# Extra TensorE products of constants at the start of each batch of a graph network with routed FFN

## The chip, the cores and the metric

The kernel runs on one core of a Trainium2 chip. The engines named here are PE (TensorE, with its weight loads as PEld), DVE (VectorE), ACT (ScalarE), POOL (GpSimd) and SP (SyncE, which issues most of the DMAs). The metric is the time on the device in microseconds (us). Three timed runs of the kernel before have a median of 739.09 us (737.73 to 739.27).

## The reference

The input x has 8 batches of 1024 rows and 128 features, and every batch has its own 1024 x 1024 adjacency matrix of zeros and ones. What is computed, cut to its core:

```
# graph layer: maximum over a row's first 25 neighbours
xn    = layernorm(x)
idx   = the first S=25 columns with adj != 0, in rising order
agg   = max over idx of xn[idx]     (also max with 0 if the row has at most 25 neighbours)
x     = x + relu(concat(xn, agg) @ W + b)

# FFN with routed experts; each tile of 128 rows has one route
h0    = layernorm(x)
h     = relu(h0 @ Wi.T + bi)
for l in 0, 1:
    h = relu(h @ Ws[l].T + bs[l]  +  h @ Wr[l, e].T + br[l, e]  +  h)    # e = the tile's route
out   = x + h @ Wo.T + bo
```

## The kernel before

**Tiling and stages.** A batch is 8 tiles of 128 rows. Tile 0, whose rows have the most neighbours, has its rows fetched by indexed DMAs that POOL issues. For the other 7 tiles (896 columns) the kernel works with slots. A slot is a group of source rows and a rank r within the group: a matrix with a one where a row's r-th neighbour of that group is (the one-hot, made by DVE or ACT from an array `rank`) is multiplied on PE with the normalised features, which are split in two parts, and DVE takes the maximum of the product with what it has (`fold_slot`, lines 959 and 961). There are 44 slots to a batch. A full slot is 4 matmuls (512 and 384 columns, for two parts), one with a group of two tiles 8, a narrow one 2.

**The order of the work.** Every engine's program walks over stages s = 0 to 9 and in each over positions p = 0 to 43 (`positions`). In stage s there run: slot p of batch s-1 (`slot`), the graph layer's end and the FFN of batch s-2 (`finish`), and masks, ranks and one-hots of batch s (`prepare`). Everything is in the order that this walk writes; an engine executes its list in that order and waits on semaphores. So there are eight stages with slots (s = 1 to 8), and in seven of them (s = 2 to 8) an FFN runs too; stage 9 has only the last batch's FFN.

**Around the change**, in a stage from 2 on:
- PE: slot p waits for its one-hot (`s_acthot` or `s_onehot`) and for the fold of slot p-2 (`s_max`), since there are two accumulators. In `finish`, position 0 turns the features (line 765), 2 to 5 hold the graph layer's product (lines 784 and 785), 12 and 13 turn h0 (line 792, waits for `s_h0` from ACT), 14 to 17 multiply with Wi (line 799, waits for ACT's copies), 19 to 34 are the two expert layers (line 815).
- DVE: the fold of slot p, then one-hots for slots 4 ahead, then its part of `finish` (the sum with x at positions 4 and 6, statistics one position later), then `norm_pair`: the layernorm chain at positions 7 and 8 (lines 980 to 991), which goes to ACT for a square root (`std`) and comes back. The fold of slot 8 stands between the halves of that chain.
- ACT: at position 7 it waits for DVE's variance, then h0 in two halves at positions 9 and 11 (line 587), copies of the turned tiles at 12 and 13 (line 593), the first layer's relu at 14 to 17 (line 597), and one-hots for slots 5 ahead in between (lines 645, 656 and 662).
- `prep_ps[0]` and `prep_ps[1]` are two PSUM banks that `prepare` uses for ranks (line 842). In stages from 1 on that is at positions 16 to 38, so that nothing is in them at the positions before. ACT reads them out (line 616) and signals `s_q`.
- `down` is a table of constants, 128 x 1024 of 16 bit, which POOL writes once at the start.

Of the kernel before, what the change touches and what calls it, by code (L numbers as in the profile page):

```python
# [15 lines left out]
P = 128  # L16
# [45 lines left out]
def gnn_ffn_program(nc, x, adj, gnn_W, gnn_b, route_id, Wi, bi, Wr, br, Ws, bs, Wo, bo, out):  # L62
    B, N, C = x.shape
    IT = N // P
# [10 lines left out]
    BANK = 512  # L75
# [8 lines left out]
    CONSTS = 7  # L84
    assert HUBS == 1 and sorted(PLACES) == [(g, r) for g in range(NG) for r in range(1, CAPS[g][0] + 1)]
    assert NW == 34 and HC == 2 and L == 2 and all(w == TT for _, _, w in SLOTS[0:2])


# [22 lines left out]
    VERDICT_AT = 24  # L111
    SPLIT_AFTER, SPLIT_BATCH = 35, 4
    FIRST_W_AT = 6
    OUT_AT = {36: 0, 39: 1}
    WEIGHTS_AT = [] + [NS + p for p in (
        0, 1, 2, 3, 4, 5, 6, 7, 9, 10, 11, 12, 14, 15, 16, 18, 19, 20, 22, 23, 24, 25,
# [14 lines left out]
    with ExitStack() as ctx:  # L131
        def sb(name, shape, dt=F32):
            return ctx.enter_context(nc.sbuf_tensor(name, shape, dt))
# [4 lines left out]
        def sem(name):  # L138
            return ctx.enter_context(nc.semaphore(name))
# [5 lines left out]
        down = sb("down", [P, N], F16)  # L145
# [74 lines left out]
        prep_f = [p[:, :].bitcast(F32) for p in prep_ps]  # L220
# [29 lines left out]
        s_q = sem("s_q")  # L250
# [61 lines left out]
        def positions():  # L312

            for s in range(B + 2):
                for p in range(NS):
                    yield s, p
# [22 lines left out]
        def weights_at(s, p, late):  # L339
            at_ = s * NS + p - late  # L340
            return [m for m in range(NW) if WEIGHTS_AT[m] == at_]
# [28 lines left out]
        def _(sp):  # L370
# [6 lines left out]
            def load_expert(k, i):  # L377

                e = sp.value_load(route[0:1, k * IT + i:k * IT + i + 1], min_val=0, max_val=NE)
                sp.dma_start(wst[:, i, :], folded[bass.ds(e, 1)].rearrange("a p w -> (a p) w")).then_inc(s_w[i], 16)  # L380
# [16 lines left out]
            for s, p in positions():  # L397
                k = s - 2
                if k == 0 and 0 <= p - FIRST_W_AT < IT:
                    if p == FIRST_W_AT:  # L400
                        sp.wait_ge(s_route, 1)
                        for i in range(NST):
                            sp.wait_ge(s_wstore[i], 16 * len(range(i, NW, NST)))
                        sp.wait_ge(s_bstore, 16)
                    load_expert(0, p - FIRST_W_AT)
                if s < B:
# [43 lines left out]
                if 0 <= k < B:  # L450
# [6 lines left out]
                    if p - 1 in LAYER_AT[1] and k + 1 < B:  # L457
                        i = LAYER_AT[1][p - 1]
                        sp.wait_ge(s_r[1], k * IT + i + 1)
                        load_expert(k + 1, i)  # L460
                    if p - 1 in OUT_AT:
                        g = OUT_AT[p - 1]
                        sp.wait_ge(s_y, 2 * k + g + 1)
# [263 lines left out]
        def _(pe):  # L727
            pe.wait_ge(s_const, CONSTS)

            def start_with_bias(bank, which):  # L730
                pe.matmul(bank, onesb[0:SPLITS, :], bias_rows[:, which].rearrange("p t c -> p (t c)"),
                          start=True, stop=False)

            def slot(b, p):
                n = b * NS + p
                g, r, wide = SLOTS[p]
                first, many = GROUPS[g]
                if p == 0:
                    pe.wait_ge(s_split, b + 1)
                if p in ACT_HOT:  # L740
                    pe.wait_ge(s_acthot, b * len(ACT_HOT) + ACT_HOT.index(p) + 1)
                else:
                    pe.wait_ge(s_onehot, b * len(DVE_HOT) + DVE_HOT.index(p) + 1)
                if n >= 2:
                    pe.wait_ge(s_max, n - 1)
                for j in range(many):
                    for part in range(PARTS):
                        for c0 in range(0, wide * P, BANK):
                            c1 = min(c0 + BANK, wide * P)
                            mm = pe.matmul(slot_ps[n % 2][:, c0:c1], xsplit[:, b % 2, part, first + j, :],  # L750
                                           onehot[:, UNIT[n] + j, c0:c1], start=(j == 0 and part == 0),
                                           stop=(j == many - 1 and part == PARTS - 1))
                mm.then_inc(s_slot, 1)

            def finish(k, p):
# [46 lines left out]
                for l in range(L):  # L802
                    if p in LAYER_AT[l]:
# [13 lines left out]
                        mm.then_inc(s_l[l], 1)  # L817
                if p in OUT_AT:
                    g = OUT_AT[p]
                    pe.wait_ge(s_r[1], k * IT + 7 + g)  # L820
# [8 lines left out]
            def prepare(s, p):  # L829
                if p in RANK_AT[s > 0]:  # L830
                    jt = RANK_AT[s > 0][p]
                    second = [f for f, many in GROUPS if many == 2 and f + 1 == jt]
                    for c in range(CHUNKS):
                        if jt == 0:
                            for i, many in enumerate(turns((s + 1) * TT)):
                                pe.wait_ge(s_turn[i], 16 * many)
                            if s > 0:
                                pe.wait_ge(s_q, 2 * IT * s - 1 + c)
                        else:
                            pe.wait_ge(s_q, 2 * IT * s + 2 * jt + c - 1)  # L840
                        cols = slice(c * CW, (c + 1) * CW)
                        mm = pe.matmul(prep_f[c][:, 0:CW], before[:, :], at[:, jt, cols],  # L842
                                       start=True, stop=not second)
                        if second:
                            mm = pe.matmul(prep_f[c][:, 0:CW], onesb[:, :], at[:, jt - 1, cols],
                                           start=False, stop=True)
                        mm.then_inc(s_rank, 1)
# [11 lines left out]
            for s, p in positions():  # L859
                if 1 <= s <= B:  # L860
                    if s == 1 and p == 0:
                        pe.wait_ge(s_biases, 1)
                    slot(s - 1, p)
                if 2 <= s:
                    finish(s - 2, p)
                if s < B:
                    prepare(s, p)
                if (s, p) == (B + 1, VERDICT_AT):
                    pe.wait_ge(s_above, 1)
                    pe.matmul(prep_f[0][0:1, 0:ROWS], above[:, 0:1], ident[0:ROWS, 0:ROWS], start=True,  # L870
                              stop=True).then_inc(s_overs, 1)
                for m in weights_at(s, p, 0):
                    if m < NIN:
                        pe.wait_ge(s_wfirst[m // 4], 16 * 4)
                    else:
                        pe.wait_ge(s_wload[m % NIN], 16 * (m // NIN))
                    if m >= 2:
                        pe.wait_ge(s_wfold, m - 1)
                    for kc in range(HC):
                        for hc in range(HC):  # L880
                            mm = pe.transpose(ffn_ps[m % 2][:, (kc * HC + hc) * P:(kc * HC + hc + 1) * P],  # L881
                                              w_in[m % NIN][:, hc, kc * P:(kc + 1) * P], ident[:, :])
                    mm.then_inc(s_wT, 1)
# [42 lines left out]
        def _(dve):  # L926
# [201 lines left out]
            def finish(k, p):  # L1128
# [9 lines left out]
                if p - 1 in SUM_AT:  # L1138
                    g = SUM_AT[p - 1]
                    dve.wait_ge(s_sum, 2 * k + g + 1)  # L1140
                    for i in range(4 * g, 4 * g + 4):
                        dve.bn_stats(stats[:, 1, i, :], x1[:, i, :])  # L1142
                if p - 1 in OUT_AT:
                    g = OUT_AT[p - 1]
                    dve.wait_ge(s_o, 2 * k + g + 1)
# [119 lines left out]
```

## Time and profile before

| | |
|---|---|
| median of 3 runs | 739.09 us |
| the profiled execution, own time | 739.0 us |
| its span | 737.3 us |
| PE busy | 612.4 us (83%) |
| DVE busy | 605.3 us (82%) |
| ACT busy | 567.5 us (77%) |
| POOL busy | 238.0 us (32%) |
| PE share of the chain that ended last | 61%, DVE 21% |
| mean granted clock of TensorE | 0.933 |

PE, DVE and ACT are busy for nearly the same time, so no average tells which one holds the others up; that has to be read stage by stage. The granted clock is given as a share of the full 2.4 GHz: 1.00 is 2.4 GHz, 0.50 is 1.2 GHz, and a value between is a stretch that held both. PE is called busy while a matmul is in flight, with an end that is modelled, so that a row's time is some tenths of a microsecond longer than the columns take.

### The profile page before, as it was taken

The numbers are of one execution on the slowest core, as the hardware profiler recorded it, in microseconds if no ns is written. First come the engines' busy times: TensorE is split into PE (matmuls) and PEld (weight loads), VectorE is DVE, ScalarE is ACT, GpSimd is POOL, SyncE is SP. The second block draws the span as 40 slices with busy tenths as digits, with TensorE's granted clock in tenths as the row PEclk, the third lists the DMA queues.
The fourth block names the chain that finished last, engine by engine and source line by source line (L and its number), as shares of the span: only waits on it lengthen the run. The fifth ranks groups of instructions, "written<-read, shape, count | busy, mean of one in ns | idle before, by whom it ended". The sixth has DMA issues, their size and how long they took to land.

```text
span 737.3 us, 11826 instructions
## 1 busy us (share of the span) xinstructions
PE 612.4 (83%) x3496; PEld 500.2 (68%) x3497; DVE 605.3 (82%) x1047; ACT 567.5 (77%) x1053; POOL 238.0 (32%) x260
## 2 busy tenths in 40 slices
PE   0463766688999799979997999899987999799786
PEld 0052545466988588858975797669875888588665
DVE  3766799988998898889988898899888988777740
ACT  5683364489998898889988998899889997488162
POOL 4522224533243332434242334333343234510000
PEclk9998798998999799979998899989998999799989
DMA  9999996479746965497639764795475553135222
GB/s 295 326 191 285 283 369 185 135 175 297 222 136 152 270 175 161 109 232 220 174 106 214 230 176 138 169 264 161 120 183 126 152 139 93 33 103 142 58 74 75
DMA packets 145171, 131.73 MB, mean 179 GB/s; under 512 B 72219, under 2 KB 112324, under 8 KB 145092
## 3 DMA queue, kind: packets, MB, share of 16 engines
q1 hardware_dynamic: 128124, 105.94, 53.5%
q0 software_dynamic: 7296, 15.74, 8.5%
q10 hardware_dynamic: 9680, 9.21, 4.4%
q8 instruction: 31, 0.51, 0.3%
q14 instruction: 40, 0.33, 0.1%
HBM read 98.20 MB, written 17.98 MB: 158 GB/s over the span
## 4 chain that ended last, share of the span: by engine, by line
PE 61%; DVE 21%; DMA 5%; issue 5%; ACT 4%; SPq 2%; DVEq 2%; ACTq 0%
PE slot_ps L750 29%; PE ffn_ps L815 15%; DVE acc L961 9%; PE prep_ps L842 3%; DMA at<-mask 3%; PE ffn_ps L799 3%; PE ffn_ps L825 2%; DMA adj_sb<-in_adj_dram 2%; PE ffn_ps L784 2%; DVE onehot L948 2%; PE ffn_ps L765 2%; DVE gath L1039 2%; DVE wst L1126 1%; PE ffn_ps L785 1%; DVE stats L1142 1%
## 5 line engine op out<-in xcount | busy, mean ns | idle before, releaser
L750 PE MATMUL slot_ps<-onehot,xsplit 128*128 128x512 f32 (+3 forms) x1376 | 373.4, 399 | 46.7 <-DVE acc L961 42.5
L961 DVE TENSOR_TENSOR acc<-slot_ps,acc 128x896 f32<-128x896 f32 (+2 forms) x336 | 293.9, 883 | 51.6 <-PE slot_ps L750 49.4
L750 PEld LDWEIGHTS slot_ps<-onehot,xsplit 128*128 128x128 f32 x1376 | 250.3, 204 | 103.2 <-issue 71.1
L530 POOL DMA_INDIRECT gath<-feature_table,idx x200 | 202.2, 1011 | 363.0 <-DMA gath<-feature_table,idx 273.5
L645 ACT ACTIVATE away<-rank,ranks 128x896 bf16<-128x896 bf16 (+3 forms) x168 | 133.0, 792 | 6.6 <-DVE wst L1126 6.3
L815 PE MATMUL ffn_ps<-hT,wst 128*128 128x128 f32 x1024 | 135.5, 277 | 0.6
L662 ACT ACTIVATE onehot<-away 128x896 fp32r<-128x896 bf16 (+3 forms) x168 | 118.7, 707 | 21.7 <-PE slot_ps L750 10.3
L815 PEld LDWEIGHTS ffn_ps<-hT,wst 128*128 128x128 f32 x1024 | 128.5, 191 | 8.2 <-issue 3.5
L604 ACT ACTIVATE hT<-ffn_ps,wst 128x128 f32<-128x128 f32 x256 | 82.4, 384 | 19.3 <-PE ffn_ps L815 17.4
L948 DVE TENSOR_SCALAR onehot<-rank,ranks 128x896 fp32r<-128x896 bf16 (+3 forms) x128 | 94.8, 741 | 2.4 <-PE slot_ps L750 2.4
L616 ACT ACTIVATE rank<-prep_ps 128x448 bf16<-128x448 f32 x128 | 63.1, 552 | 22.6 <-PE prep_ps L842 10.6
L656 ACT ACTIVATE onehot<-rank,ranks 128x896 fp32r<-128x896 bf16 (+1 forms) x56 | 66.0, 1179 | 11.4 <-PE slot_ps L750 10.7
L689 ACT ACTIVATE mask<-adj_sb 128x1024 bf16<-128x1024 uint32 x56 | 58.0, 1046 | 16.2 <-DMA at<-mask 12.1
L842 PE MATMUL prep_ps<-at,before 128*128 128x448 bf16 x128 | 40.3, 384 | 15.9 <-DMA at<-mask 12.3
L881 PE MATMUL ffn_ps<-ident,hT 128*128 128x128 f32 x136 | 24.9, 314 | 33.7 <-DVE wst L1126 31.3
L881 PEld LDWEIGHTS ffn_ps<-ident,hT 128*128 128x128 f32 x136 | 17.9, 162 | 43.2 <-issue 42.1
L1020 DVE MAX8 top<-score 128x8 f32<-128x1024 f32 x32 | 39.1, 1220 | 0.3
L799 PE MATMUL ffn_ps<-xnT,wiT 128*128 128x512 f32 x64 | 33.3, 608 | 0.2 <-ACT xnT L593 0.2
L842 PEld LDWEIGHTS prep_ps<-at,before 128*128 128x128 bf16 x128 | 11.4, 99 | 32.1 <-DMA at<-mask 11.7
L825 PE MATMUL ffn_ps<-woT,hT 128*128 128x128 f32 x256 | 32.8, 281 | 0.0
L825 PEld LDWEIGHTS ffn_ps<-woT,hT 128*128 128x128 f32 x256 | 29.8, 191 | 3.6 <-issue 3.6
L515 POOL TENSOR_TENSOR xsplit<-xn,xsplit 128x1024 fp32r<-128x1024 f32 x8 | 19.2, 2400 | 38.7 <-DVE acc L961 31.2
(120 smaller groups left out, 541.9 us busy)
## 6 DMA issues: line engine op xcount, KB each, us to landing
wst<-folded_weights SPq DMA_DIRECT2D x128, 257.0 KB, 2.9
adj_sb<-in_adj_dram SPq DMA_DIRECT2D x64, 512.0 KB, 5.9
folded_weights<-wst ACTq DMA_DIRECT2D x34, 256.0 KB, 5.8
hT<-in_L_ffn_Wr_dram SPq DMA_DIRECT2D x26, 256.0 KB, 8.8
xs<-in_x_dram SPq DMA_DIRECT2D x8, 512.0 KB, 8.0
feature_table<-xn SPq DMA_DIRECT2D x8, 512.0 KB, 4.2
x<-in_x_dram SPq DMA_DIRECT2D x8, 512.0 KB, 4.2
out_dram<-h SPq DMA_DIRECT2D x16, 256.0 KB, 2.5
```

Source lines behind the costliest of these rows:

```text
L530: pool.indirect_dma_start(gath[:, j, :], None, tables[b], bass.IndirectOffsetOnAxis(ap=idx[:, b % 2, h, j:j + 1], axis=0)).then_inc(signal ...
L604: ins = act.activation(hT[:, 1 - l, j, i, :], ffn_ps[(i + 1) % 2][:, j * P:(j + 1) * P], ACT.Relu, bias=wst[:, i, HC * HID + j:HC * HID + ...
L616: act.activation(rank[:, s % 2, jt, c * CW:(c + 1) * CW], prep_f[c][:, 0:CW], ACT.Copy, bias=float(NONE)).then_inc(s_q, 1)
L645: act.activation(away[:, i % AWAYS, 0:wide * P], rank[:, b % 2, first, 0:wide * P], ACT.Square, bias=ranks[:, r - 1:r], scale=-1.0).then_i ...
L656: act.activation(onehot[:, UNIT[n]:UNIT[n] + many, 0:wide * P], rank[:, b % 2, first:first + many, 0:wide * P], ACT.Relu, bias=ranks[:, 1: ...
L662: act.activation(onehot[:, UNIT[n], 0:wide * P], away[:, i % AWAYS, 0:wide * P], ACT.Relu, bias=1.0, scale=-1.0).then_inc(s_acthot, 1)
L750: mm = pe.matmul(slot_ps[n % 2][:, c0:c1], xsplit[:, b % 2, part, first + j, :], onehot[:, UNIT[n] + j, c0:c1], start=(j == 0 and part == ...
L815: mm = pe.matmul(ffn_ps[(i + 1) % 2][:, j * P:(j + 1) * P], wst[:, i, c0:c0 + P], hT[:, l, kc, i, :], start=(kc == 0), stop=(kc == HC - 1))
L825: mm = pe.matmul(o, hT[:, 0, kc, i, :], woT[:, kc, :], start=False, stop=(i % 4 == 3 and kc == HC - 1))
L842: mm = pe.matmul(prep_f[c][:, 0:CW], before[:, :], at[:, jt, cols], start=True, stop=not second)
L948: dve.tensor_scalar(onehot[:, UNIT[n]:UNIT[n] + many, 0:wide * P], rank[:, b % 2, first:first + many, 0:wide * P], ranks[:, r - 1:r], None ...
L961: dve.tensor_tensor(acc[:, p % 2, 0:cols], slot_ps[n % 2][:, 0:cols], acc[:, p % 2, 0:cols], ALU.max).then_inc(s_max, 1)
```

## The change

At positions 5 to 11 of the stages 2 to 8, ahead of the position's slot, PE multiplies a 128 x 128 piece of `down` with a 128 x 512 piece of it into `prep_ps[0]`: 2, 4, 5, 5, 4, 3 and 2 times, 25 in a stage. Nobody reads the result. The first of them waits for `s_q`, that is, for ACT to have read the last ranks of the stage before. In stage 9 there are 24 such matmuls at positions 6 to 11, behind `finish`. Together they are 7 x 25 + 24 = 199.

```
+    BUSY_AT = {5: 2, 6: 4, 7: 5, 8: 5, 9: 4, 10: 3, 11: 2}
+    BUSY_AT_END = {6: 4, 7: 4, 8: 4, 9: 4, 10: 4, 11: 4}
...
+            def keep_busy(s, p):
+
+                where = BUSY_AT if s < B + 1 else BUSY_AT_END
+                if p == min(where):
+                    pe.wait_ge(s_q, 2 * IT * min(s, B))
+                for _ in range(where.get(p, 0)):
+                    pe.matmul(prep_f[0][:, 0:BANK], down[:, 0:P], down[:, 0:BANK], start=True, stop=True)
...
                 if 1 <= s <= B:
                     if s == 1 and p == 0:
                         pe.wait_ge(s_biases, 1)
+                    if s >= 2:
+                        keep_busy(s, p)
                     slot(s - 1, p)
                 if 2 <= s:
                     finish(s - 2, p)
+                if s == B + 1:
+                    keep_busy(s, p)
```

Lines below the new ones have moved: in the kernel after, 750 is 760, and 784, 785 and 792 are 794, 795 and 802.

PE's program before, in a stage from 2 on, from the slot of position 5 to that of position 8 (784 and 785 are the graph layer, 750 the slots):

```order
L750 MATMUL slot_ps<-onehot,xsplit 128x512 [waits s_max,s_onehot]
L750 MATMUL slot_ps<-onehot,xsplit 128x384
L750 MATMUL slot_ps<-onehot,xsplit 128x512
L750 MATMUL slot_ps<-onehot,xsplit 128x384
L784 MATMUL ffn_ps<-gw,xnT 128x128
L785 MATMUL ffn_ps<-gw,aggT 128x128
L784 MATMUL ffn_ps<-gw,xnT 128x128
L785 MATMUL ffn_ps<-gw,aggT 128x128
L750 MATMUL slot_ps<-onehot,xsplit 128x384 [waits s_max,s_acthot]
L750 MATMUL slot_ps<-onehot,xsplit 128x384
L750 MATMUL slot_ps<-onehot,xsplit 128x512 [waits s_max,s_onehot]
```

The same place now, from the graph layer of position 5 to the start of slot 8 (742 is a product of constants):

```order
L794 MATMUL ffn_ps<-gw,xnT 128x128
L795 MATMUL ffn_ps<-gw,aggT 128x128
L742 MATMUL prep_ps<-down 128x512 x4
L760 MATMUL slot_ps<-onehot,xsplit 128x384 [waits s_max,s_acthot]
L760 MATMUL slot_ps<-onehot,xsplit 128x384
L742 MATMUL prep_ps<-down 128x512 x5
L760 MATMUL slot_ps<-onehot,xsplit 128x512 [waits s_max,s_onehot]
L760 MATMUL slot_ps<-onehot,xsplit 128x384
L760 MATMUL slot_ps<-onehot,xsplit 128x512
L760 MATMUL slot_ps<-onehot,xsplit 128x384
L742 MATMUL prep_ps<-down 128x512 x5
L760 MATMUL slot_ps<-onehot,xsplit 128x512 [waits s_max,s_acthot]
```

Ahead of slots 6, 7 and 8 there now stand 4, 5 and 5 matmuls; two more stand ahead of slot 5, above this piece.

PE's program in stage 9, from the graph layer's last products to the turning of h0, before:

```order
L784 MATMUL ffn_ps<-gw,xnT 128x128
L785 MATMUL ffn_ps<-gw,aggT 128x128
L792 MATMUL ffn_ps<-ident,h 128x128 [waits s_h0]
L792 MATMUL ffn_ps<-ident,h 128x128 x3
L792 MATMUL ffn_ps<-ident,h 128x128 [waits s_h0]
```

And now:

```order
L795 MATMUL ffn_ps<-gw,aggT 128x128
L742 MATMUL prep_ps<-down 128x512 [waits s_q]
L742 MATMUL prep_ps<-down 128x512 x23
L802 MATMUL ffn_ps<-ident,h 128x128 [waits s_h0]
L802 MATMUL ffn_ps<-ident,h 128x128 x3
```

All 24 stand in one piece, behind the graph layer and ahead of the wait for h0. No other engine's program changes.

## Rows read from the trace of the kernel before

**Rows 1.** The page: granted TensorE clock in 40 slices, in tenths.
```profile
PEclk9998798998999799979998899989998999799989
```
**Rows 2.** Chain of waits, start and length in us: position 0 of three stages.
```profile
382.67 1.74 PE ffn_ps L765 x16
...
460.61 1.74 PE ffn_ps L765 x16
...
537.71 1.74 PE ffn_ps L765 x16
```
**Rows 3.** Busy time and clock (ninth column) by 2 us, stage from 382.67.
```profile
398.00:400.00 2.00, 0.48 (x1) 0.50 (x2) 1.77 (x6) 1.59 (x4) 0.62 (x1) 0.83 1.25 281
400.00:402.00 2.00, 1.90 (x6) 1.15 (x4) 1.78 (x6) 1.56 (x4) 1.27 (x2) 0.50 1.02 327
...
408.00:410.00 2.00, 2.00 (x9) 1.76 (x8) 1.51 (x2) 2.00 (x5) 0.54 (x1) 0.61 1.05 377
```
**Rows 4.** Timeline of DVE, folds of slots 5, 6, 7 and 8.
```profile
392.55 1.09 DVE L961 TENSOR_TENSOR acc<-slot_ps,acc 128x896 f32<-128x896 f32 x1 [0.80 <-PE slot_ps L750]
...
394.34 0.54 DVE L961 TENSOR_TENSOR acc<-slot_ps,acc 128x384 f32<-128x384 f32 x1
...
395.40 1.08 DVE L961 TENSOR_TENSOR acc<-slot_ps,acc 128x896 f32<-128x896 f32 x1
...
398.29 1.08 DVE L961 TENSOR_TENSOR acc<-slot_ps,acc 128x896 f32<-128x896 f32 x1
```
**Rows 5.** Timeline of DVE, fold of slot 13 in stages 2 to 8.
```profile
174.33 1.09 DVE L961 TENSOR_TENSOR acc<-slot_ps,acc 128x896 f32<-128x896 f32 x1 [1.92 <-PE slot_ps L750]
...
252.31 1.09 DVE L961 TENSOR_TENSOR acc<-slot_ps,acc 128x896 f32<-128x896 f32 x1 [1.81 <-PE slot_ps L750]
...
330.41 1.09 DVE L961 TENSOR_TENSOR acc<-slot_ps,acc 128x896 f32<-128x896 f32 x1 [1.80 <-PE slot_ps L750]
...
408.49 1.09 DVE L961 TENSOR_TENSOR acc<-slot_ps,acc 128x896 f32<-128x896 f32 x1 [2.02 <-PE slot_ps L750]
...
485.60 1.09 DVE L961 TENSOR_TENSOR acc<-slot_ps,acc 128x896 f32<-128x896 f32 x1 [1.35 <-PE slot_ps L750]
...
563.35 1.09 DVE L961 TENSOR_TENSOR acc<-slot_ps,acc 128x896 f32<-128x896 f32 x1 [2.00 <-PE slot_ps L750]
...
641.61 1.09 DVE L961 TENSOR_TENSOR acc<-slot_ps,acc 128x896 f32<-128x896 f32 x1 [2.69 <-PE slot_ps L750]
```
**Rows 6.** Timeline of PE in the same stage: slots 6+7, 10+11, 12; Wi; ranks.
```profile
393.16 1.68 PE L750 MATMUL slot_ps<-onehot,xsplit 128*128 128x384 f32 x6
...
399.52 2.59 PE L750 MATMUL slot_ps<-onehot,xsplit 128*128 128x512 f32 x6 [2.31 <-DVE acc L961]
403.63 0.98 PE L750 MATMUL slot_ps<-onehot,xsplit 128*128 128x384 f32 x2 [1.52 <-DVE acc L961]
...
409.67 1.02 PE L799 MATMUL ffn_ps<-xnT,wiT 128*128 128x512 f32 x2
...
413.88 0.54 PE L842 MATMUL prep_ps<-at,before 128*128 128x448 bf16 x2
```
**Rows 7.** Line 842 from 412 to 417 us, ns minimum/median/maximum.
```profile
L842 PE MATMUL prep_ps<-at,before x4: 352/352/363, 413.9 to 417.0; 128*128 128x448 bf16 x4
```
**Rows 8.** Timeline of ACT in the same stage: square root, copy of turned h0.
```profile
398.41 0.22 ACT L678 ACTIVATE std<-mv 128x16 f32<-128x16 f32 x1 [2.50 <-DVE mv L986]
...
408.03 0.58 ACT L593 ACTIVATE xnT<-ffn_ps 128x512 f32<-128x512 f32 x1
```
**Rows 9.** Timeline of PE in stage 9.
```profile
702.41 1.11 PE L792 MATMUL ffn_ps<-ident,h 128*128 128x128 f32 x4 [6.19 <-ACT h L587]
...
703.95 1.12 PE L792 MATMUL ffn_ps<-ident,h 128*128 128x128 f32 x4 [0.42 <-ACT h L587]
```
**Rows 10.** Busy time and clock by 2 us in stage 9.
```profile
704.00:706.00 2.00, 2.00 (x6) 1.45 (x7) 1.43 (x7) 0.98 (x2) 0.00 (x0) 0.50 0.00 0
706.00:708.00 2.00, 2.00 (x4) 0.54 (x4) 1.70 (x5) 1.07 (x2) 0.00 (x0) 0.87 0.01 4
```

## The prediction

> **What bounds the kernel now.** I read the page's clock line first. It dips about once every four slices, so once a stage [rows 1]. The table by 2 us then places a dip: in the stage that begins at 382.67 us the clock is whole until inside 398 to 400, at half from there, and whole again inside 408 to 410 [rows 3]. From the shares 0.83 and 0.61 the half rate lasts from 399.3 to 409.6 us. Just before the fall PE had waited 2.31 us, and in the half-rate stretch it waits another 1.52 us, both times for DVE's folds [rows 6].
>
> The timeline of DVE shows who pays. DVE waits 0.80 us ahead of the fold of slot 5, then works without a gap until it waits 2.02 us for slot 13, which PE was computing at half rate [rows 4, 5]. After that it is busy nearly without a gap through the middle of the stage. So in stages 2 to 7 a late fold 13 is a late stage. The trace has a test of this: the stage from 460.61 has the shortest wait there, 1.35 us [rows 5], and lasts 537.71 - 460.61 = 77.10 us against 460.61 - 382.67 = 77.94 for the one before it [rows 2]. What is saved ahead of fold 13 is kept. The six waits of stages 2 to 7 are 1.92, 1.81, 1.80, 2.02, 1.35 and 2.00, together 10.9 us, and stage 8 has 2.69 [rows 5].
>
> **What an added matmul costs.** No row shows this one. The nearest is line 842: two 16-bit matmuls of 448 columns take 0.54 us, one takes 0.35 [rows 6, 7], so the second begins 0.19 us after the first, and 512 columns take 0.19 x 512/448 = 0.217 us at the whole clock. At half rate it would be twice that. The range for one is 0.21 (512 columns at 2.4 GHz) to 0.43. I take 0.217; weight loads of 16 bit lie beside the matmul before.
>
> **Part 1: the 25 in stages 2 to 7.** They stand ahead of each slot's waits, so where PE would wait for DVE they fill the wait, and where PE was in time they make the slot late. I follow the stage from 382.67.
> - Fold 5 was already waiting for PE. Two matmuls make it 0.43 us late: 392.98.
> - Slot 7 ended at 393.16 + 1.68 = 394.84. Ahead of it now stand 2 + 4 + 5 = 11 matmuls, 2.38 us. The six matmuls of slots 6 and 7 have 2560 columns, 1.07 us at 2.4 GHz; of the 0.6 us left about 0.3 is a wait for fold 5 (to 392.55 + 1.09 = 393.64), which the matmuls cover. So slot 7 ends at 394.84 + 2.38 - 0.3 = 396.9, and fold 7 starts at 397.0 in place of 395.40: 1.6 us late.
> - The five ahead of slot 8 end at 396.7 + 1.08 = 397.8, slot 8 needs some 1.0 and is done at 398.8. Fold 8 now comes at 398.29 + 1.6 = 399.9, so it isn't delayed further. The same holds for 9 to 11: 4, 3 and 2 matmuls run inside waits of PE.
> - DVE has no gap from fold 5 to fold 12, so all that follows is 1.6 us late, and it is ready for fold 13 at 408.49 - 2.02 + 1.6 = 408.1.
> - With the clock whole, PE ends slot 13 at about 407.7: slot 12 starts behind fold 10, now at 403.63 [rows 6] and then at 405.2; its own 768 columns take 0.33, the turning of h0 0.43, and 1.5 + 0.2 for the eight matmuls of slot 13. So fold 13 starts at 408.1 in place of 408.49.
>
> A stage so gains its wait less 1.6 us: over six stages 10.9 - 9.6 = 1.3 us.
>
> Against it stands ACT. Its square root waits for DVE [rows 8] and is 1.6 us late too, and ACT has no gap behind it, so the copy of turned h0 begins at 409.6 and ends at 410.2 in place of 408.6. PE's line 799 then starts at 410.25, not 409.67 [rows 6]. Followed on through line 799, this makes slot 17 about 0.25 us late for DVE; behind it the order has slack again. Six times 0.25 is 1.5 us. Part 1 with a whole clock is therefore 1.5 - 1.3 = +0.2 us: what the clock gives, the late norm takes.
>
> **Part 2: the 25 in stage 8.** There DVE and ACT have less to do and PE bounds the rest of the stage. DVE is ready for fold 13 at 641.61 - 2.69 + 1.6 = 640.5; PE comes at about 640.7. Gain 0.9 us.
>
> **Part 3: the 24 in stage 9.** PE waits 6.19 us for h0 [rows 9]; 24 x 0.217 = 5.2 us lie inside that wait, and they cost nothing (at the half rate they would take 10.4 and cost 4). With the clock whole, what ran at half rate from 703.95 until inside 706 to 708 (share 0.87, so until 706.5) [rows 9, 10] takes half: 2.55/2, about 1.25 us gained, since all behind it hangs on it.
>
> **Part 4: a clock that falls all the same.** Slot 10 waits for the end of fold 8 (399.9 + 1.1 = 401.0) and takes 0.8, the two matmuls behind it 0.43: 402.2. From there to slot 12 at 405.2 PE has only slot 11's two small matmuls, a hole of 3.0 us. It is like those of 2.31 and 1.52 us ahead of and behind the falls now [rows 6]. When it does make the clock fall, that is at about 405 to 406, and slots 12 and 13 and the turning of h0 (2.3 us of work) run at half rate for the most part: fold 13 is then some 1.1 us later than in part 1, and since that takes away ACT's 0.25, the stage costs 0.85 more. I give a fall 4 in 10 in each of seven stages: 2.8 x 0.85 = +2.4 us.
>
> Waits and queues: the new wait for s_q is met, since ACT's last rank of a stage is at position 38 and this is position 5 of the next. POOL, SP and DMAs get no instruction. The masks of positions 7, 9 and 10 are up to 1.6 us later with ACT, and their transposes; the ranks that need them are at 413.88 [rows 6], some 3 us behind.
>
> **Sum.** 739.0 (the profiled execution, 737.3 of span and 1.7 around it; 0.1 under the median) + 0.2 - 0.9 - 1.25 + 2.4 = 739.4 us.
>
> **Two rules of the Trainium skill.** In the trace the clock is at half for about 10 us a stage after PE's waits [rows 3, 6]. The page TensorE: Matmul & The Clock Gate (What's actually happening) says that the throttled state is the default and that activity releases it. By that the added work would hold the clock in every stage and the sum loses part 4: 737.0. The rows can't show whether products nobody needs count.
> The trace shows slots in program order. The same page (Part 2, on weight loads) says that matmuls stay in program order and only weight loads are pulled ahead; by that the eleven ahead of slot 7 are all paid, as in part 1. If they gave way, the 9.6 us and the 1.5 would go.
>
> **The rivals.**
> - *The clock never falls.* For: stage 460.61 kept what it saved. Against: the hole at 402.2. Time: 739.0 + 0.2 - 0.9 - 1.25 = 737.0; with ACT's 0.25 not arising, 735.5. If the matmuls also lay wholly in waits (fold 5's wait of 0.80 and gapless DVE speak against it), 10.9 + 2.7 + 1.25 would go: 724.
> - *Slower: the matmuls ahead of slot 7 push back DVE's norm chain and with it ACT by more than the fold-13 wait is worth.* The place is slots 5 to 7, the price (delay - wait) a stage. It decides from a delay of about 2 us. A matmul of 0.25 us, or 0.1 us each time PE turns between 16-bit and 32-bit work, makes the delay 1.9 to 2.0 (0.35 x 6: +2 us); with falls in more than half of the stages, +1 more: 742. At 0.43 us each the delay would be 1.6 + 2.4 = 4.0 us, six times 4.0 - 1.8: 752.
> - *No effect of the matmuls on the clock.* Falls stay where they were, and slot 12 with all behind it is 1.6 us late at the same rate: 739.0 + 7 x 1.6 = 750. Nothing in the trace speaks for it, but it doesn't show such products either.
>
> **How the numbers follow.** Forecast (delay 1.6, falls in some stages): 0.43, its own range 738 to 741. Clock never falls: 0.27 (737, to 735.5), fully free 0.03. Longer delay: 0.22 (742). No effect on the clock: 0.05. The range 735.8 to 742.5 leaves out the far cases. About 0.2% (1.5 us) is what a measurement of this kernel can tell from no change. Below 737.6: the free case, most of the cases in which the clock never falls and a few of the forecast's, 0.31. Above 740.6: 0.05 + 0.22 and a share of the forecast's upper end, 0.29. Between: 0.40.
>
> **What would show it.** In the profile after: fold 7 about 4.0 us behind the start of fold 5 in place of 395.40 - 392.55 = 2.85 [rows 4], fold 13 with a wait under 0.3 us where the clock holds; ACT's std wait 4.1 us instead of 2.5; line 742 at 0.22 us each; the clock whole in stage 9, and its products with Wi over 1.25 us earlier. The forecast is wrong if fold 7 is not late (then far faster), if the clock line has a dip in each stage still (slower), or if DVE has new waits behind fold 13.

## The result and the profile after

The kernel after takes 743.88 us (median of 9 runs, 740.87 to 746.84), the kernel before 739.09 us (median of 9, 736.87 to 741.72). The ratio is 1.0065 with a 95% interval of 1.004 to 1.009: slower, by 3.0 to 6.6 us. The forecast of 739.4 us and its range up to 742.5 were wrong. The profiled execution of the kernel after is the fastest of its nine, 740.87 us with a span of 739.1. Four executions of the experiments' timings took between 910 and 2022 us, in a slow state of the chip, and are left out of every ratio.

The page of the kernel after, its clock line and two groups of matmuls (the added ones and the product with Wi):

```profile
PEclk9986898999999999999999999999999999999999
...
L742 PE MATMUL prep_ps<-down 128*128 128x512 f16 x199 | 51.5, 381 | 0.0
...
L809 PE MATMUL ffn_ps<-xnT,wiT 128*128 128x512 f32 x64 | 33.1, 605 | 7.1 <-ACT xnT L595 4.7
```

Against [rows 1] the dips are gone from stage 2 on: in this execution the 199 matmuls hold the clock. But line 809 (799 before) now has 7.1 us of idle time in front of it, where the kernel before had 0.2.

The chain of waits of the kernel after: position 0 of stages 2 to 9, each row the start of a stage.

```profile
147.74 1.74 PE ffn_ps L775 x16
226.48 1.74 PE ffn_ps L775 x16
305.21 1.73 PE ffn_ps L775 x16
383.92 1.73 PE ffn_ps L775 x16
462.48 1.74 PE ffn_ps L775 x16
541.06 1.73 PE ffn_ps L775 x16
619.39 1.74 PE ffn_ps L775 x16
692.11 1.75 PE ffn_ps L775 x16
```

The same view of the kernel before, the three starts that [rows 2] doesn't show and that bound the stretches compared here:

```profile
226.67 1.74 PE ffn_ps L765 x16
...
615.52 1.73 PE ffn_ps L765 x16
688.96 1.75 PE ffn_ps L765 x16
```

Three stretches come out of the two. Stages 3 to 7: 619.39 - 226.48 = 392.91 us against 615.52 - 226.67 = 388.85, so +4.06, or 0.81 a stage. Stage 8: 72.72 against 73.44, so -0.72. From the start of stage 9 to the end of the span: 46.95 against 48.31, so -1.36. Of the stretches compared, only the middle stages lose.

DVE in the stage from 383.92, folds 5, 6, 7, 8, 13, 15, 17 and 19 of the kernel after:

```profile
394.22 1.09 DVE L975 TENSOR_TENSOR acc<-slot_ps,acc 128x896 f32<-128x896 f32 x1 [1.23 <-PE slot_ps L760]
396.31 0.56 DVE L975 TENSOR_TENSOR acc<-slot_ps,acc 128x384 f32<-128x384 f32 x1 [0.23 <-PE slot_ps L760]
398.23 1.09 DVE L975 TENSOR_TENSOR acc<-slot_ps,acc 128x896 f32<-128x896 f32 x1 [0.76 <-PE slot_ps L760]
401.13 1.08 DVE L975 TENSOR_TENSOR acc<-slot_ps,acc 128x896 f32<-128x896 f32 x1
...
409.05 1.08 DVE L975 TENSOR_TENSOR acc<-slot_ps,acc 128x896 f32<-128x896 f32 x1
...
413.43 1.09 DVE L975 TENSOR_TENSOR acc<-slot_ps,acc 128x896 f32<-128x896 f32 x1 [0.25 <-PE slot_ps L760]
...
417.16 1.09 DVE L975 TENSOR_TENSOR acc<-slot_ps,acc 128x896 f32<-128x896 f32 x1 [0.32 <-PE slot_ps L760]
...
420.87 1.09 DVE L975 TENSOR_TENSOR acc<-slot_ps,acc 128x896 f32<-128x896 f32 x1 [0.42 <-PE slot_ps L760]
```

From fold 5 to fold 7 it is 4.01 us, where [rows 4] have 2.85, and fold 5's own wait is 1.23 where it was 0.80: together 1.6 us. Fold 8 follows without a wait. Fold 13 has no wait, where [rows 5] have 2.02. Then there are three waits for PE, 0.25, 0.32 and 0.42, together 0.99 us (0.72 to 0.92 in the other five of stages 2 to 7). The kernel before has none at these folds in the same stage; its folds 15, 17, and 18 with 19:

```profile
412.55 1.09 DVE L961 TENSOR_TENSOR acc<-slot_ps,acc 128x896 f32<-128x896 f32 x1
...
415.87 1.09 DVE L961 TENSOR_TENSOR acc<-slot_ps,acc 128x896 f32<-128x896 f32 x1
...
418.06 2.08 DVE L961 TENSOR_TENSOR acc<-slot_ps,acc 128x896 f32<-128x896 f32 x2
```

PE in that stage, timeline of the kernel after (slot 12, the second turning of h0, and the product with Wi):

```profile
406.29 0.58 PE L760 MATMUL slot_ps<-onehot,xsplit 128*128 128x384 f32 x2 [1.65 <-DVE acc L975]
...
409.27 0.65 PE L802 MATMUL ffn_ps<-ident,h 128*128 128x128 f32 x4 [0.32 <-ACT h L589]
...
411.45 1.12 PE L809 MATMUL ffn_ps<-xnT,wiT 128*128 128x512 f32 x2 [1.18 <-ACT xnT L595]
```

ACT in the same stage, square root and copy of the turned h0:

```profile
401.25 0.22 ACT L680 ACTIVATE std<-mv 128x16 f32<-128x16 f32 x1 [4.11 <-DVE mv L1000]
...
410.83 0.58 ACT L595 ACTIVATE xnT<-ffn_ps 128x512 f32<-128x512 f32 x1
```

ACT waits 4.11 us for the norm where [rows 8] have 2.50: the 1.6 us again. From the square root to the copy it takes 9.6 us in both kernels (401.25 to 410.83; 398.41 to 408.03), so it catches nothing up. PE waits 1.18 us for the copy, and line 809 starts 27.5 us into the stage (411.45 - 383.92), where it was 27.0 (409.67 - 382.67). (Counted from the first fold it is 26.05 us here, and 24.4 to 25.5 over stages 2 to 7 of the kernel before.) From there PE's timeline has no gap until past slot 19: PE is what DVE waits for.

PE in stage 9 of the kernel after:

```profile
699.20 5.34 PE L742 MATMUL prep_ps<-down 128*128 128x512 f16 x24
705.56 0.66 PE L802 MATMUL ffn_ps<-ident,h 128*128 128x128 f32 x4 [1.01 <-ACT h L589]
707.10 0.66 PE L802 MATMUL ffn_ps<-ident,h 128*128 128x128 f32 x4 [0.88 <-ACT h L589]
```

The 24 matmuls take 5.34 us, 0.22 each, inside the wait for h0, which still has 1.01 us left of the 6.19 of [rows 9].

### The profile page after: what moved, and what is told of

It reads as the page before. It is cut to its first block, busy times and chain, and to the rows that moved or that the text cites. A ratio compares the mean times of both kernels' runs of the same rounds, so it can differ in the third digit from the quotient of the medians.

```text
span 739.1 us, 12224 instructions
## 1 busy us (share of the span) xinstructions
PE 630.9 (85%) x3695; PEld 503.1 (68%) x3696; DVE 607.3 (82%) x1047; ACT 565.9 (77%) x1053; POOL 237.6 (32%) x260
## 4 chain that ended last, share of the span: by engine, by line
PE 63%; DVE 17%; ACT 7%; issue 5%; DMA 4%; DVEq 2%; SPq 1%; ACTq 0%
PE slot_ps L760 28%; PE ffn_ps L825 14%; DVE acc L975 7%; PE ffn_ps L809 4%; PE prep_ps L852 3%; ACT h L589 3%; PE ffn_ps L835 2%; PE ffn_ps L794 2%; PE prep_ps L742 2%; DMA at<-mask 2%; PE ffn_ps L795 2%; PE ffn_ps L775 2%; ACT mask L691 2%; DMA adj_sb<-in_adj_dram 2%; DVE wst L1140 2%
## 5 line engine op out<-in xcount | busy, mean ns | idle before, releaser
L760 PE MATMUL slot_ps<-onehot,xsplit 128*128 128x512 f32 (+3 forms) x1376 | 362.7, 389 | 29.4 <-DVE acc L975 24.6
L760 PEld LDWEIGHTS slot_ps<-onehot,xsplit 128*128 128x128 f32 x1376 | 241.9, 194 | 80.8 <-issue 50.1
L658 ACT ACTIVATE onehot<-rank,ranks 128x896 fp32r<-128x896 bf16 (+1 forms) x56 | 66.0, 1179 | 11.5 <-PE slot_ps L760 10.7
L852 PE MATMUL prep_ps<-at,before 128*128 128x448 bf16 x128 | 40.2, 384 | 15.0 <-DMA at<-mask 11.4
L742 PE MATMUL prep_ps<-down 128*128 128x512 f16 x199 | 51.5, 381 | 0.0
L680 ACT ACTIVATE std<-mv 128x16 f32<-128x16 f32 (+1 forms) x10 | 2.1, 214 | 43.8 <-DVE mv L1000 39.0
L852 PEld LDWEIGHTS prep_ps<-at,before 128*128 128x128 bf16 x128 | 11.4, 99 | 30.8 <-DMA at<-mask 11.5
```

The source lines that it names most:

```text
L658: act.activation(onehot[:, UNIT[n]:UNIT[n] + many, 0:wide * P], rank[:, b % 2, first:first + many, 0:wide * P], ACT.Relu, bias=ranks[:, 1: ...
L742: pe.matmul(prep_f[0][:, 0:BANK], down[:, 0:P], down[:, 0:BANK], start=True, stop=True)
```

## The experiments

Each kernel was timed beside runs of the kernel before on the same chip; the ratio is to those. Not all experiments ran on the same chip: the runs of the kernel before have medians of 739.7 us beside the first four, 739.1 beside the next four and 737.3 beside the last two, so kernels of different groups are compared by ratio or by stages and not by their times alone. "Line 809" is the start of the product with Wi behind the first fold of its stage, "the stage" the distance of such first folds; both are typical of stages without a fall of the clock. The theories: **A**, the 11 matmuls ahead of slot 7 delay DVE's norm chain by 1.6 us, ACT with it, and PE waits for ACT; **B**, the early matmuls are what holds the clock; **C**, any added matmul costs.

**Late products only.**

```
-    BUSY_AT = {5: 2, 6: 4, 7: 5, 8: 5, 9: 4, 10: 3, 11: 2}
+    BUSY_AT = {8: 5, 9: 4, 10: 3, 11: 2}
```

> The products at positions 5, 6 and 7 are left out, those at 8 to 11 and in stage 9 stay. Theory A (the 11 products ahead of slot 7 make DVE's norm chain 1.6 us late, ACT with it, and PE then waits 1.2 us for ACT's copy of the turned h0): fold 7 is back at 11.2 us behind the stage's first fold, PE's wait at line 809 is gone, and if the clock still holds the stage is about 1.8 us shorter than in the kernel before (DVE's wait for slot 13 goes): 6 x 1.8 + 1.5 + 1.25, about 727 us. Theory B (the early products are what holds the clock): fold 7 is in time, but the clock falls once a stage again, and the time is that of the kernel before less the end, 738 us. Theory C (any added product costs, wherever it stands): over 741 us.

734.03 us, ratio 0.9937 (0.9908 to 0.9966): faster than the kernel before. The fold of slot 13 comes without a wait, and line 809 still waits for ACT. Timeline of DVE, then of PE, in the stage from 383.70 (first fold at 385.19):

```profile
407.44 1.07 DVE L975 TENSOR_TENSOR acc<-slot_ps,acc 128x896 f32<-128x896 f32 x1
```

```profile
409.63 1.12 PE L809 MATMUL ffn_ps<-xnT,wiT 128*128 128x512 f32 x2 [1.17 <-ACT xnT L595]
```

Fold 7 is back at 11.2 us behind the first fold, line 809 starts at 24.4 in place of 26.05, and the stages are 76.7 to 77.4 us in place of 78.3 to 78.75. Removing 11 matmuls a stage moved fold 7 and line 809 by the same 1.6 us. C falls, since 14 a stage stay, and B for the most part: the clock is whole in four of seven stages without the early products. A is right on the delay, but wrong on one point: the wait at line 809 did not go. It is 1.17 us here too, because PE and ACT's copy are both 1.6 us earlier; with the clock held, it is ACT's copy that sets line 809. So the time came out 7 us above the 727 of A (whose own sum, taken from 739.1, gives 725.5). The clock fell in stages 4, 6 and 7, each time ahead of slot 12, for one stretch of 3.4 us. Busy time and clock of this kernel by 2 us (clock in the ninth column):

```profile
326.00:328.00 2.00, 0.92 (x5) 0.91 (x6) 2.00 (x4) 2.00 (x4) 0.59 (x1) 0.90 0.59 131
328.00:330.00 2.00, 2.00 (x8) 1.81 (x7) 1.92 (x3) 2.00 (x6) 1.70 (x2) 0.50 0.82 156
330.00:332.00 2.00, 2.00 (x10) 1.55 (x9) 0.65 (x1) 2.00 (x5) 0.04 (x1) 0.74 1.07 168
```

**Early products only.**

```
-    BUSY_AT = {5: 2, 6: 4, 7: 5, 8: 5, 9: 4, 10: 3, 11: 2}
+    BUSY_AT = {5: 2, 6: 4, 7: 5}
```

> The products at positions 8 to 11 are left out, those at 5 to 7 and in stage 9 stay. Theory A: the delay of 1.6 us at fold 7 and PE's wait for ACT stay whole, and the clock may fall again behind position 8; stages of 78.7 us or more, and with falls 79.5: 744 to 749 us. Theory B: the clock holds as in the kernel after, and the time is the same within 1 us. Theory C: 14 fewer products in seven stages give back about 14 x 0.217 x 7 = 21 us at most; anything under 740 us would speak for it.

746.84 us, ratio 1.0115 (1.008 to 1.0149), inside A's range. Fold 7 is at 12.8 us, and the clock falls in each of stages 2 to 8, so B falls here too. Chain of waits, the longest stage's start and the next:

```profile
227.91 1.74 PE ffn_ps L775 x16
307.64 1.74 PE ffn_ps L775 x16
```

That stage is 79.73 us long; stages 2 to 7 take 78.4 to 79.7. The delay without the held clock is worse than either kernel.

**Stage 9 only.**

```
-                    if s >= 2:
+                    if s >= B + 2:
                         keep_busy(s, p)
```

> Only the 24 products in stage 9 stay; the stages 2 to 8 are as before. Theory A: stages like before (about 78.0 us, clock falls in each), the end shorter by the half-rate stretch: 1.25 us under the kernel before. Theory C: no gain or a loss of up to 4 us there.

738.09 us, ratio 0.9987 (0.9964 to 1.0009). The stages are like before (76.9 to 78.05), and from the start of stage 9 to the end it is 736.1 - 689.04 = 47.1 us against 48.3. Its row in the chain of waits:

```profile
689.04 1.75 PE ffn_ps L775 x16
```

The time alone can't tell 1.2 us from nothing; the stretch in the profile shows it.

**ACT's normalised tiles later, in the kernel after.**

```
-             [11, 13, 14, 16]]
+             [13, 14, 16, 17]]
```

> The kernel after, with ACT's four pairs of normalised tiles moved from positions 11, 13, 14 and 16 to 13, 14, 16 and 17, so that one pair (0.87 us) no longer stands between h0 and the copies of the turned h0. Theory A (the loss is PE's wait for ACT's copy at line 809): the copy starts 0.8 us earlier, the wait of 1.2 us shrinks to about 0.4, and each of six stages is about 0.7 us shorter: 4 us under the kernel after. Rival (DVE's 1.6 us are the loss by themselves, or PE is full anyway): no change within 1 us.

742.81 us, ratio 1.0053 (1.0023 to 1.0084), 1.1 us under the kernel after. The median is unclear, the profile isn't. Chain of waits, starts of stages 2 to 5:

```profile
148.30 1.74 PE ffn_ps L775 x16
226.37 1.73 PE ffn_ps L775 x16
305.36 1.74 PE ffn_ps L775 x16
383.46 1.74 PE ffn_ps L775 x16
```

Stages 2 and 4 are 78.07 and 78.10 us, against 78.7 in the kernel after: 0.6 less (0.7 was expected), and line 809 starts at 25.3 in place of 26.05. The wait for ACT went from 1.18 to 0.41 us. PE in stage 4:

```profile
332.13 1.12 PE L809 MATMUL ffn_ps<-xnT,wiT 128*128 128x512 f32 x2 [0.41 <-ACT xnT L595]
```

The stage between them is 78.99, because here the clock fell in stages 3, 5, 7 and 8 (in none in the kernel after), each time ahead of slot 12 for 3.4 us. So a fall costs 0.9 us here (0.7 in stage 5, whose length is 78.81), and in stage 8, whose length is 74.00 us against 72.7 in the kernel after, 1.3. A move of ACT's operations, which changes the program of neither PE nor DVE, gains what it takes from ACT's path: this is the run that shows ACT in the path. That the clock would fall in four stages was not foreseen. They have all 25 products of the kernel after, so these do not hold the clock in every case; why it fell here stays open.

**Late products and six at position 12.**

```
-    BUSY_AT = {5: 2, 6: 4, 7: 5, 8: 5, 9: 4, 10: 3, 11: 2}
+    BUSY_AT = {8: 5, 9: 4, 10: 3, 11: 2, 12: 6}
```

> Products at positions 8 to 11 as in the kernel after (5, 4, 3, 2), none at 5 to 7, and 6 more at position 12, ahead of slot 12, where PE waits 1.65 us for DVE's fold 10; stage 9 as in the kernel after. Theory A with falls priced at 0.85 us each (the clock fell for 3.4 us in three stages of the run with late products, each time in the hole ahead of slot 12): no fall in any stage from 2 on, all stages near 77.0 us, 1 to 3 us under the run with late products alone, 731 to 733 us. Rival (6 x 0.217 = 1.3 us more in front of slot 12 push slot 13 back): DVE waits for slot 13 and the time is that of late products or above.

732.46 us, ratio 0.9915 (0.9878 to 0.9951). No fall from stage 2 on, and stages of 76.7 to 77.2 us. Timeline of PE:

```profile
407.95 1.13 PE L809 MATMUL ffn_ps<-xnT,wiT 128*128 128x512 f32 x2 [1.17 <-ACT xnT L595]
```

Line 809 starts at 24.45 and waits for ACT as before. The three falls of the run with late products cost it only some 0.4 us in all: its stages with a fall take 77.40, 77.07 and 76.73 us, the same ones here 77.13, 76.97 and 76.72. PE had the wait for ACT to spare (it is down to 0.12 to 0.24 us in those stages). So the gain of the six is small, and the intervals of the two ratios overlap.

**Narrow products.**

```
-                    pe.matmul(prep_f[0][:, 0:BANK], down[:, 0:P], down[:, 0:BANK], start=True, stop=True)
+                    pe.matmul(prep_f[0][:, 0:P], down[:, 0:P], down[:, 0:P], start=True, stop=True)
```

> The kernel after with every product cut from 512 to 128 columns, the same count (25 a stage, 24 in stage 9). Theory A (the delay is the columns streamed ahead of slot 7): one product takes about 0.06 us, the 11 ahead of slot 7 about 0.6 us less the 0.3 of wait that they cover, so that fold 7 is 0.1 to 0.5 us late in place of 1.6. With so little work the clock falls once a stage as before: about 738 to 741 us. Rival (a fixed price for each product, whatever its width): fold 7 stays 1.6 us late, and the time is 745 us or more.

741.72 us, ratio 1.0032 (1.0006 to 1.0058), 0.7 above the expected. Fold 7 is at 11.4 us behind the first fold, 0.17 late: the price is the columns, not the count. The clock fell once in each of stages 2 to 8 and in stage 9 (mean 0.929), so these products hold nothing. In the profiles stages 2 to 8 take 540.2 us, as in the kernel before; the end behind them takes 49.9 against 48.5 (both from the first product of line 775, 765 before). The fall in stage 9 begins 3 us later there, at 702.6 us in place of 699.7, and so lies over more of the work behind the wait for h0; that this is the whole loss was not tested.

**ACT's normalised tiles later, in the kernel before** (the edit of the fourth experiment, no products).

> The kernel before, with ACT's pairs of normalised tiles moved from positions 11, 13, 14 and 16 to 13, 14, 16 and 17 and no products. Theory A: PE is behind ACT there because of the half-rate slot 13, so ACT's copy is not what it waits for, and nothing changes: within 1 us of the kernel before. Rival (moving the pairs is a gain by itself): 3 us or more under the kernel before.

738.89 us, ratio 0.9994 (0.9968 to 1.002). Nothing changes, as A has it: without the held clock PE is late at line 799 by itself, and ACT's copy isn't waited for.

**The kernel after again.**

> The kernel after, once more, for a second profile and for times beside the others. Its profiled run had no fall in stages 2 to 9 and is 3 us under the median of its runs. If that difference is falls in the hole ahead of slot 12 (0.85 us each), this profile is either again without falls near 741 us, or shows falls of 3.4 us behind position 11 and stages of 79.4 to 79.6 us with them. If it is anything else, stages without a fall are longer than 78.8 us.

743.8 us, ratio 1.0062 (1.0033 to 1.009). Chain of waits, starts of stages 2, 3, 8 and 9:

```profile
151.18 1.74 PE ffn_ps L775 x16
229.68 1.74 PE ffn_ps L775 x16
...
622.69 1.74 PE ffn_ps L775 x16
695.39 1.75 PE ffn_ps L775 x16
```

Its span is 742.5 us, 3.4 above the other profile's, and no clock fall lies in stages 2 to 8, nor in stage 9 before its last microseconds. From stage 2 to the end it is 591.3 us in both. The whole difference of the two executions lies ahead of stage 2 (151.18 against 147.74), where there are no products. Neither of the two explanations in the expectation holds.

**Late products with 12, and ACT's tiles later.** Both edits together.

> Late products with 6 at position 12, and ACT's pairs of normalised tiles at positions 13, 14, 16 and 17. Theory A (with the clock held, the stage is as long as the start of line 809, the product with Wi, is late, and that waits for ACT's copy): the start goes from 24.45 us behind the stage's first fold to about 23.7, and the stages from 77.0 to 76.2 to 76.5 us: 728 to 730 us. Rival (DVE, without a gap from fold 5 to fold 14, is the bound once the delay is gone): line 809 starts earlier and the stages stay at 76.9 to 77.1 us, 732 us.

730.29 us (median of 6), ratio 0.9896 (0.9863 to 0.993), the lowest ratio here; its interval overlaps that of the kernel without ACT's move. PE in the stage from 376.12 (first fold at 377.62):

```profile
401.55 1.13 PE L809 MATMUL ffn_ps<-xnT,wiT 128*128 128x512 f32 x2 [0.40 <-ACT xnT L595]
```

Line 809 starts at 23.65 in most stages (23.93 in this one) and the stages are 76.2 to 76.7 us, in place of 24.45 and 76.7 to 77.2. Stage by stage it is 0.3 to 0.6 us, 2.8 us over the six. The wait for ACT went from 1.17 to 0.4 us. The profiled execution has a span of 723.7 us, 7.0 below that of the kernel without the move; 4.3 of this is that stage 2 starts at 146.4 in place of 150.7, so that its stages are what is compared.

**Late products with 12, and the five of position 7.**

```
-    BUSY_AT = {5: 2, 6: 4, 7: 5, 8: 5, 9: 4, 10: 3, 11: 2}
+    BUSY_AT = {7: 5, 8: 5, 9: 4, 10: 3, 11: 2, 12: 6}
```

> Late products with 6 at position 12, and the five of position 7 as well (none at 5 and 6). Theory A: slot 7 was done 0.55 us ahead of its fold and had about 0.3 us of wait, so of the 5 x 0.217 = 1.08 us about 0.2 to 0.3 us reach fold 7, which starts at 11.4 to 11.5 us behind the stage's first fold; the start of line 809 and the stages are later by the same amount, 77.2 to 77.3 us, and the time is 1 to 2 us above that of late products with 12. Rival (the first products ahead of fold 7 cost in full, or the price is not linear in the delay): fold 7 is 1 us late, and the time 738 us or more.

734.28 us, ratio 0.9947 (0.9926 to 0.9968). DVE's timeline, fold 7:

```profile
394.97 1.09 DVE L975 TENSOR_TENSOR acc<-slot_ps,acc 128x896 f32<-128x896 f32 x1 [0.23 <-PE slot_ps L760]
```

Fold 7 is 0.32 us late (11.54 against 11.22), line 809 0.3 (24.77) and the stages 0.3 (77.0 to 77.5), so of 1.08 us of matmuls 0.32 reached the path. Six times 0.3 is 1.8 us; the ratio is 0.0032 higher (2.4 us), with intervals that overlap. In this profile the clock also fell once in stage 9, for 3.4 us, in spite of the 24 products there.

The kernels in which the clock held (in the fourth row in stages 2, 4 and 6 alone), side by side (us behind the stage's first fold, and stages 2 to 7 without a fall):

| kernel | fold 7 | line 809 | stage | median | ratio |
|---|---|---|---|---|---|
| late, with 12, ACT's tiles later | 11.2 | 23.65 | 76.2 to 76.7 | 730.3 | 0.9896 |
| late, with 12 | 11.2 | 24.45 | 76.7 to 77.2 | 732.5 | 0.9915 |
| from 7, with 12 | 11.5 | 24.77 | 77.0 to 77.5 | 734.3 | 0.9947 |
| after, ACT's tiles later | 12.8 | 25.3 | 78.1 | 742.8 | 1.0053 |
| after | 12.8 | 26.05 | 78.3 to 78.75 | 743.9 | 1.0065 |

The later line 809, the longer the stage, whether the delay was made by PE (fold 7) or by ACT. The kernel before does not lie on this line (24.4 to 25.5 with stages of 77.1 to 78.0): there slot 13, computed at half rate, is what DVE waits for.

## Why the prediction was wrong

- **The price of a matmul:** right. 0.217 was taken, 0.22 measured (5.34 us for 24). The slower rival's extra 0.1 us at each turn between 16-bit and 32-bit work would have made the delay at fold 7 1.9 us or more; it was 1.6.
- **The delay of the eleven ahead of slot 7:** right, 1.6 us predicted and measured, in DVE (11.2 to 12.8) and in ACT's wait (2.50 to 4.11). The narrow products and those from position 7 on show that the price is the time of the columns beyond PE's spare time.
- **Fold 13:** right. It was to start at 408.1 - 382.67 = 25.4 us into the stage; it did at 409.05 - 383.92 = 25.1. So DVE was 0.7 us earlier there than in the kernel before, in spite of the delay; 0.4 was forecast.
- **The step that failed** is the one behind it, "this makes slot 17 about 0.25 us late for DVE; behind it the order has slack again". Line 809 was forecast well (410.25 - 382.67 = 27.6, measured 27.5). What was wrong is the slack. PE has no gap from line 809 until past slot 19, and DVE waits for it at slots 15, 17 and 19, 0.25 + 0.32 + 0.42 = 0.99 us in place of 0.25. The working took DVE for the bound of the middle of the stage where PE and DVE share it. With it falls "What is saved ahead of fold 13 is kept": in this stage fold 13 is 0.7 us early and the stage 0.6 us longer (78.57 against 77.95 from first fold to first fold). The test on the stage from 460.61 could not show this, since line 799 was early there too (24.4 us behind the first fold, against 25.5 in the stage before it). Part 1 was put at +0.2 us for six stages; measured it is +4.06 for five of them, and +4.9 for six. DVE's waits give -10.9 + 9.6 + 5.1 (the new waits in six stages) = +3.8 of it; the last 1.1 us is not accounted for by them. The prediction had named the sign of its own failure, "new waits behind fold 13", and that is the one that came.
- **Stage 8 and stage 9:** the terms were -0.9 and -1.25, measured -0.72 and -1.36. Right in the main.
- **Falls of the clock (part 4):** +2.4 us was the term, and no fall is in the 14 stages 2 to 8 of two profiles of the kernel after. At 4 in 10 a stage that would be rare, so the chance was too high for this kernel, though other executions were not profiled. The place was right where falls happened, ahead of slot 12 and 3.4 us long, in three stages of the run with late products and four of the run with ACT's tiles later. The price (0.85 us) was right in stages 3 and 5 of the latter, 0.9 and 0.7; it was 1.3 in its stage 8, and 0.3 or less with late products, where PE had the wait for ACT to spare.
- **The sum:** with the measured terms, 739.0 + 4.9 - 0.7 - 1.4 = 741.8. Two terms were wrong in opposite directions and hid each other in the forecast of 739.4. The medians differ by 4.8 us, and the interval of the ratio (+3.0 to +6.6 us) just leaves out +2.8. The two profiled executions differ by 740.87 - 739.0 = 1.9, as +2.8 and a stage 2 that starts about 1 us earlier in the kernel after would have it. What is left of the medians, up to 2 us, is open: the time ahead of stage 2 differs by 3.4 us between two executions of one and the same kernel, no run here tells whether the change moves its mean, and falls in executions without a profile are not ruled out.
- **The rival that came true** is the slower one. Its path, DVE's norm chain and ACT with it, is the one found, but its price was not: it was to decide from a delay of about 2 us, and 1.6 was enough. That point was computed against DVE's wait for slot 13 alone.
- **The two rules of the Trainium skill** (TensorE: Matmul & The Clock Gate). That activity releases the throttle (What's actually happening) agrees with the wide products of the kernel after: the clock stayed whole in stages 2 to 8 of both profiles, and fell as before with narrow ones. That the added work would thereby hold the clock in every stage, as the prediction drew from it, came true in this kernel and not in others: with ACT's tiles later it fell in four stages with the same 25 products. Even where it held, the forecast of 737.0 that hung on it did not come. The rule that matmuls stay in program order (Part 2) agrees too: the eleven ahead of slot 7 were paid, 1.6 us at fold 7.

## What to carry to other kernels

Work that only keeps a clock up must stand where its engine waits anyway. Here the same idea was 4.8 us slower with 11 of its 25 matmuls in front of a slot that had 0.55 us to spare, and about 5 us faster without these 11 (0.9937), 6 us with six more inside a later wait (0.9915). Where three engines are busy to 80%, follow a delay through each of them to the place where it meets the others again, past the first meeting: a wait removed ahead of it is worth only what the next engine in the order, here ACT's copy, lets through.

## What was not expected of the hardware

- Products of constants that nobody reads can hold the clock of TensorE: 25 of 512 columns and 16 bit in a stage took the mean granted clock from 0.933 to 0.975 and left no fall in stages 2 to 8 of two profiles. The same 25 with 128 columns left it at 0.929. It is no guarantee: with only ACT's operations moved, the clock fell in four stages in spite of the 25.
- With the late products the clock fell for one stretch of 3.4 us, 19 to 21 us behind the stage's first fold. In the kernel before it fell at 14 to 17 us and stayed down for 6.8 or 10.2 us, and PE waited for DVE inside the half-rate stretch as well (1.52 us in [rows 6]). That this wait kept it down was not tested.
- Two executions of one kernel differ by 3.4 us of 740 before stage 2 begins, and by less than 0.1 us in the 591 us behind it. Five of their six stage lengths agree within 0.12 us and that of stage 2 within 0.3. So a change of 0.3 us in each of six stages (products from position 7) can be told from the stages of one profile each, where single times don't tell it.
